# Zero-tile matmuls in TensorE's waits, a new order of the norm columns, and a value product in row halves

## What is computed

```
x_dct = DCT over w and h of the normalised x
blocks of 8 x 8 frequencies, 64 of them per image:
    q, k, v = tokens @ Wq, Wk, Wv          (4 heads of 16)
    q, k    = each divided by its norm over the block's 64 positions
    attn    = softmax(q k^T * rescale);  x_low = (attn v) @ proj_w + proj_b
h1     = gelu(1x1 conv(x_dct)); h1 = gelu(3x3 depthwise conv(h1)); x_conv = h1 + x_dct
x_high = gelu(1x1 conv(x_conv)) + x_conv
x      = x + inverse DCT(coef * x_low + (1 - coef) * x_high + x_dct)
t      = tokens of x (4096 of 64 numbers), layer norm
router = softmax(t @ Wr + br), top 2 of 8 experts, weights from their gap
t      = t + sum over experts of gate * (gelu(LN(t) @ W1 + b1) @ W2 + b2)
```

## Time and profile before

| | before |
|---|---|
| median of three executions | 278.15 us (277.07 to 278.45) |
| the profiled execution | 280.61 us, its span 278.4 us |
| TensorE busy | 247.1 us, 89% of the span |
| VectorE, ScalarE, GpSimd busy | 53%, 47%, 16% |
| mean granted clock of TensorE | 0.936 of full speed |
| DMA | 13.42 MB, 48 GB/s over the span |

### The profile page before, as it was taken

How to read it: one execution, slowest core, us unless ns; L and a number is a source line. 1 busy time by engine, 2 the same in 40 slices (tenths; PEclk the granted TensorE clock), 3 DMA queues, 4 the chain that set the end, 5 groups by cost and what they waited for, 6 DMA issues and landing times.

```text
span 278.4 us, 3222 instructions
## 1 busy us (share of the span) xinstructions
PE 247.1 (89%) x1238; PEld 134.8 (48%) x1238; DVE 146.7 (53%) x264; ACT 130.2 (47%) x206; POOL 45.4 (16%) x45
## 2 busy tenths in 40 slices
PE   3678789999996796896898979999999999999994
PEld 3564579956844464596795223222232333333331
DVE  0780938884359797187597344433344433334444
ACT  1336641003062244405616746555665665666660
POOL 3930067003085006400330000000000000000000
PEclk9955999999999799998955999999999999999998
DMA  7920000000000000000000861507060523215000
GB/s 242 237 44 0 2 0 4 0 0 0 2 0 0 1 0 0 2 0 0 2 0 13 181 129 46 105 0 190 0 151 2 128 60 93 61 55 133 1 2 38
DMA packets 6143, 13.42 MB, mean 48 GB/s; under 512 B 2672, under 2 KB 4080, under 8 KB 5104
## 3 DMA queue, kind: packets, MB, share of 16 engines
q1 hardware_dynamic: 6128, 13.21, 20.1%
HBM read 12.03 MB, written 1.18 MB: 47 GB/s over the span
## 4 chain that ended last, share of the span: by engine, by line
PE 70%; DVE 16%; ACT 6%; DMA 5%; issue 1%; SPq 0%; DVEq 0%
PE psum L636 21%; PE psum L621 20%; PE psum L451 5%; PE psum L469 3%; PE psum L441 3%; PE psum L513 3%; DMA wide<-gate_store 3%; DVE place L978 2%; PE psum L408 2%; PE psum L538 2%; PE psum L477 2%; PE psum L391 2%; DVE place L962 2%; ACT place L671 1%; PE psum L556 1%
## 5 line engine op out<-in xcount | busy, mean ns | idle before, releaser
L778 ACT ACTIVATE hid<-psum,b1p 128x512 f32<-128x512 f32 x128 | 77.9, 688 | 43.3 <-PE psum L621 43.3
L621 PE MATMUL psum<-tok,w1s 128*128 128x512 f16 x256 | 64.7, 390 | 0.0
L636 PE MATMUL psum<-hid,w 128*64 128x512 f32 x256 | 61.8, 604 | 2.0 <-DVE term L1062 2.0
L1062 DVE SCALAR_TENSOR_TENSOR term<-psum,sm,wide 128x512 f32<-128x512 f32 x32 | 24.0, 750 | 73.0 <-PE psum L636 68.0
L621 PEld LDWEIGHTS psum<-tok,w1s 128*128 128x128 f16 x256 | 21.9, 100 | 51.3 <-ACT hid L778 26.6
L636 PEld LDWEIGHTS psum<-hid,w 128*64 128x64 f32 x256 | 15.6, 136 | 34.0 <-issue 26.6
L1067 DVE TENSOR_TENSOR x<-x,term 128x512 f32<-128x512 f32 x32 | 22.1, 692 | 1.1
L469 PE MATMUL psum<-h_pad,tap_bd 128*128 128x512 f32 x36 | 15.8, 592 | 0.0
L451 PE MATMUL psum<-wide,c 128*128 128x128 f32 x64 | 14.4, 396 | 0.0
L451 PEld LDWEIGHTS psum<-wide,c 128*128 128x128 f32 x64 | 13.1, 205 | 1.3 <-issue 0.5
L906 DVE SCALAR_TENSOR_TENSOR place<-h_pad,sm,place 128x512 f32<-128x512 f32 x16 | 12.0, 752 | 0.6
(11 more groups left out here) (135 smaller groups left out, 325.8 us busy)
## 6 DMA issues: line engine op xcount, KB each, us to landing
wide<-gate_store SPq DMA_DIRECT2D x16, 512.0 KB, 6.3
xs<-in_x SPq DMA_DIRECT2D x2, 512.0 KB, 5.0
w1f<-in_W SPq DMA_DIRECT2D x2, 512.0 KB, 8.9
block_out<-x SPq DMA_DIRECT2D x4, 256.0 KB, 6.6
w<-in_W SPq DMA_DIRECT2D x1, 512.0 KB, 11.2
c<-const SPq DMA_DIRECT2D x1, 483.5 KB, 4.3
sm<-in_small SPq DMA_DIRECT2D x1, 419.0 KB, 5.2
gate_store<-gate_rows SPq DMA_DIRECT2D x2, 64.0 KB, 5.5
```

The costliest lines, as they stand in the source:

```text
L621: mm = pe.matmul(h_bank(n), w1s[:, part, e, k * P:(k + 1) * P], tok[:, pair, half, b, :], start=part == 0, stop=part == 1)
L636: mm = pe.matmul(y_bank(u)[b * H:(b + 1) * H, :], w2[:, e * KT + k, :], hid[:, u % 2, B2 * k + b, :], start=k == 0, stop=k == KT - 1)
L778: act.activation(hid[:, u % 2, t, :], h_bank(n), ACT.Gelu, bias=b1p[:, e * KT + k:e * KT + k + 1]).then_inc(gelu_ready, 1)
L1062: dve.scalar_tensor_tensor(term[:, u % 2, :], y_bank(u), b2t[:, e:e + 1], gate_b[part][:, e % (E // 2), :], ALU.add, ALU.mult).then_inc(te ...
```

## The change

There are three edits.

**Holds.** A tile `still` of 128 x 512 fp16 is zeroed as GpSimd's first instruction. `hold_clock(count, where)` on TensorE issues `count` matmuls of that tile with itself, 512 columns each, into a bank that holds nothing needed at that point. They stand ahead of the waits of `dct_over_h` (7 for pair 0, after a wait for the zeroed tile, 6 for pair 1), `dct_over_w(0)` (8), `windows(0)` (6), `conv_in(0)` (6), `norms_of_k(1)` (8, with its two waits in the other order and the holds between them), `inverse_over_kh(1)` (6), both `features` (5 each) and both `gates_to_rows` (5 each). The last have new waits ahead of the holds: for the normalised tokens, and for pair 0 also for `bias_ready`, since the bank is the one in which the sums of `bias` lie.

**Norm columns.** The columns of Wq and Wk were ordered (which, head, depth), and are now ordered (depth, which, head). With that `prod` has the eight columns of one depth side by side, and `norms` reads runs of eight floats, 128 apart, where it read single floats 16 apart. ScalarE's `keep_tk` now reads PSUM with a step of eight floats, and `diagonal` for `wq_bd` reads its source with such a step.

**Value product.** `wv_rep` holds Wv on all rows, 128 x 128 in place of two such tiles, and `times_wv` multiplies the lower 64 rows and the upper 64 rows by themselves, each into its bank, where it multiplied all 128 rows with zeros in one half.

```diff
@@ -117,7 +117,7 @@
 
 SMALL = {}
 at = 0
-for name, n in (("wqk", 2 * HD), ("proj", HEADS * C), ("c1a", C), ("c2", C), ("wv_t", 2 * C), ("taps", 9), ("proj_b", 1),
+for name, n in (("wqk", 2 * HD), ("proj", HEADS * C), ("c1a", C), ("c2", C), ("wv_t", C), ("taps", 9), ("proj_b", 1),
                 ("rescale", HEADS), ("ln_g", E), ("ln_b", E), ("b1", NT), ("b2", E), ("wr", E), ("br", E),
                 ("coef", H * K)):
     SMALL[name] = slice(at, at + n)
@@ -132,14 +132,12 @@
     def put(name, v):
         v = v.reshape(v.shape[0], -1)
         out[:, SMALL[name]] = np.tile(v, (P // v.shape[0], 1))
-    put("wqk", np.concatenate([a["L0_conv_Wq"], a["L0_conv_Wk"]], axis=1))
+    both = np.stack([a["L0_conv_Wq"].reshape(C, HEADS, DH), a["L0_conv_Wk"].reshape(C, HEADS, DH)], axis=1)
+    put("wqk", both.transpose(0, 3, 1, 2))
     put("proj", a["L0_conv_proj_w"].reshape(HEADS, DH, C).transpose(1, 0, 2))
     put("c1a", a["L0_conv_c1a_w"].reshape(C, C).T)
     put("c2", a["L0_conv_c2_w"].reshape(C, C).T)
-    wv = np.zeros((2, HD, 2, C), np.float32)
-    for odd in range(2):
-        wv[odd, :, odd] = a["L0_conv_Wv"].T
-    put("wv_t", wv.reshape(P, 2 * C))
+    put("wv_t", a["L0_conv_Wv"].T)
     put("taps", a["L0_conv_c1b_w"].reshape(C, 9))
     put("proj_b", a["L0_conv_proj_b"].reshape(C, 1))
     put("rescale", a["L0_conv_rescale"].reshape(1, HEADS))
@@ -194,7 +192,7 @@
 
         def weight(name):
             return sm[:, SMALL[name]]
-        wqk = weight("wqk").rearrange("p (a n) -> p a n", a=2)
+        wqk = weight("wqk")
         proj = weight("proj").rearrange("p (h c) -> p h c", h=HEADS)
         c1a, c2, wv_t, taps_w = weight("c1a"), weight("c2"), weight("wv_t"), weight("taps")
         lng, lnb, b1t, b2t = weight("ln_g"), weight("ln_b"), weight("b1"), weight("b2")
@@ -203,7 +201,7 @@
         proj_bd = sb("proj_bd", [P, HEADS, P])
         conv_bd = sb("conv_bd", [P, 4, P])
         tap_bd = sb("tap_bd", [P, 9, P])
-        wv_rep = sb("wv_rep", [P, 2, P])
+        wv_rep = sb("wv_rep", [P, P])
         coef_rest = sb("coef_rest", [P, CHUNK])
         w1f = sb("w1f", [P, E, HID])
         w1g = sb("w1g", [P, E, HID])
@@ -216,6 +214,7 @@
         xs = sb("xs", [P, PAIRS, N])
         x1 = sb("x1", [P, PAIRS, N])
         tok = sb("tok", [P, PAIRS, 2, B2, TT // 2 * P], F16)
+        still = sb("still", [P, CHUNK], F16)
         gate_rows = sb("gate_rows", [P, PAIRS, P])
         h_pad = sb("h_pad", [P, PAIRS, B2, H + 2, K + 2])
         place = [sb(f"place{n}", [P, PAIRS, N]) for n in range(6)]
@@ -246,7 +245,7 @@
         spread_k = [wide[0][:, p, 0:N] for p in range(PAIRS)]
         y_sb = [wide[0][:, p, 0:N] for p in range(PAIRS)]
         y_t = [wide[0][:, p, N:2 * N] for p in range(PAIRS)]
-        prod = [wide[1][:, p, :].rearrange("p (g a n) -> p g a n", a=2, n=HD) for p in range(PAIRS)]
+        prod = [wide[1][:, p, :].rearrange("p (g n) -> p g n", n=P) for p in range(PAIRS)]
         mix = [wide[1][:, p, :].rearrange("p (g n) -> p g n", n=P) for p in range(PAIRS)]
 
 
@@ -290,6 +289,7 @@
         const_in, const16_in, weights_in = sem("const_in"), sem("const16_in"), sem("weights_in")
         ffn_in, out_done = sem("ffn_in"), sem("out_done")
         dve_chain, pool_chain = sem("dve_chain"), sem("pool_chain")
+        still_zero = sem("still_zero")
         pad_zero, bd_ready, w1_ready = sem("pad_zero"), sem("bd_ready"), sem("w1_ready")
         conv_bd_ready = sem("conv_bd_ready")
         bias_t, bias_ready, wr_ready = sem("bias_t"), sem("bias_ready"), sem("wr_ready")
@@ -373,8 +373,18 @@
         def _(pe):
 
 
+            def hold_clock(count, where):
+
+                for _ in range(count):
+                    pe.matmul(where, still[:, 0:P], still[:, 0:where.shape[1]], start=True, stop=True)
+
             def dct_over_h(p):
 
+                if p == 0:
+                    pe.wait_ge(still_zero, 1)
+                    hold_clock(7, bank(slot(1, 1), 0))
+                if p:
+                    hold_clock(6, bank(slot(1, 1), 0))
                 pe.wait_ge(x_in[p], 16)
                 pe.wait_ge(dct_in, 16)
                 for cp in range(CP):
@@ -384,6 +394,8 @@
 
             def dct_over_w(p):
 
+                if p == 0:
+                    hold_clock(8, bank(slot(1, 1), 0))
                 pe.wait_ge(const_in, 16)
                 for cp in range(CP):
                     if cp % 4 == 0:
@@ -434,11 +450,10 @@
             def gram_times_w(p):
 
                 pe.wait_ge(weights_in, 16)
-                wqk_all = wqk[:, :, :].rearrange("p a n -> p (a n)")
                 for g in range(G):
                     if g % K == 0:
                         pe.wait_ge(gram_ready, 2 * p + g // K + 1)
-                    mm = pe.matmul(slot(p, g // K)[:, g % K * P:(g % K + 1) * P], gram[p][:, parity(g), :], wqk_all, start=True, stop=True)
+                    mm = pe.matmul(slot(p, g // K)[:, g % K * P:(g % K + 1) * P], gram[p][:, parity(g), :], wqk, start=True, stop=True)
                     if g % K == K - 1:
                         mm.then_inc(t_done, 1)
 
@@ -446,9 +461,9 @@
 
                 pe.wait_ge(tk_ready, 2 * p + 1)
                 pe.wait_ge(prod_ready, 2 * (p + 1))
-                columns = prod[p].rearrange("p g a (h d) -> p d (g a h)", d=DH)
+                columns = prod[p].rearrange("p g (d n) -> p d g n", d=DH)
                 for d in range(DH):
-                    mm = pe.matmul(slot(p, 0)[:, 0:2 * G * HEADS], const("pick")[:, DH - 1 - d:DH - 1 - d + P], columns[:, d, :],
+                    mm = pe.matmul(slot(p, 0)[:, 0:2 * G * HEADS], const("pick")[:, DH - 1 - d:DH - 1 - d + P], columns[:, d, :, :],
                                    start=d == 0, stop=d == DH - 1)
                 mm.then_inc(norms_done, 1)
 
@@ -471,8 +486,10 @@
 
             def norms_of_k(p):
 
+                pe.wait_ge(second_dconv_ready, p + 1)
+                if p:
+                    hold_clock(8, bank(slot(p, 0), 1))
                 pe.wait_ge(spread_ready, p + 1)
-                pe.wait_ge(second_dconv_ready, p + 1)
                 for j in range(2):
                     mm = pe.matmul(slot(p, 0)[:, j * CHUNK:(j + 1) * CHUNK], mask, spread_k[p][:, j * CHUNK:(j + 1) * CHUNK],
                                    start=True, stop=True)
@@ -510,8 +527,9 @@
                 for j in range(2):
                     pe.wait_ge(yt_ready, 2 * p + j + 1)
                     for odd in range(2):
-                        mm = pe.matmul(slot(p, j)[:, odd * CHUNK:(odd + 1) * CHUNK], wv_rep[:, odd, :],
-                                       y_t[p][:, j * CHUNK:(j + 1) * CHUNK], start=True, stop=True)
+                        of = slice(odd * HD, (odd + 1) * HD)
+                        mm = pe.matmul(slot(p, j)[:, odd * CHUNK:(odd + 1) * CHUNK], wv_rep[of, :],
+                                       y_t[p][of, j * CHUNK:(j + 1) * CHUNK], start=True, stop=True)
                     mm.then_inc(mix_done, 1)
 
             def low(p):
@@ -533,6 +551,8 @@
 
             def inverse_over_kh(p):
 
+                if p:
+                    hold_clock(6, bank(slot(0, 1), 0))
                 pe.wait_ge(back_ready, 2 * (p + 1))
                 for cp in range(CP):
                     mm = pe.matmul(slot(p, 0)[:, cp * P:(cp + 1) * P], back[p][:, cp * P:(cp + 1) * P], idct_h, start=True, stop=True)
@@ -559,6 +579,7 @@
 
             def features(p):
 
+                hold_clock(5, bank(slot(p, 1), 0))
                 pe.wait_ge(const16_in, 16)
                 to = slot(p, 1).bitcast(F16)
                 for j in range(TT):
@@ -585,6 +606,11 @@
 
             def gates_to_rows(p):
 
+                pe.wait_ge(xn_ready, 2 * (p + 1))
+                if p == 0:
+                    pe.wait_ge(bias_ready, 1)
+                pe.wait_ge(xn_ready, 2 * (p + 1))
+                hold_clock(5, bank(slot(p, 0), 1))
                 pe.wait_ge(gparts_ready, p + 1)
                 pe.transpose(slot(p, 0)[:, P:2 * P], gates[:, p].rearrange("p j b e t -> p (j b e t)"), ident).then_inc(gates_done, 1)
 
@@ -693,7 +719,7 @@
                 for j in range(2):
                     act.wait_ge(prod_ready, 2 * p + j + 1)
                     act.copy(tk[p].rearrange("p (h g e) -> p g h e", h=HEADS, e=DH)[:, j * K:(j + 1) * K, :, :],
-                             slot(p, j).rearrange("p (g a h e) -> p g a h e", a=2, h=HEADS, e=DH)[:, :, 1, :, :]).then_inc(tk_ready, 1)
+                             slot(p, j).rearrange("p (g e a h) -> p g a h e", a=2, h=HEADS, e=DH)[:, :, 1, :, :]).then_inc(tk_ready, 1)
 
             def gelu_depthwise(p):
                 act.wait_ge(first_taps_done, p + 1)
@@ -786,6 +812,7 @@
 
         @block.gpsimd
         def _(pool):
+            pool.memset(still[:, :], 0.0).then_inc(still_zero, 1)
             pool.memset(h_pad[:, :, :, :], 0.0).then_inc(pad_zero, 1)
             pool.wait_ge(const_in, 16)
             pool.wait_ge(weights_in, 16)
@@ -801,14 +828,12 @@
```

(12 more changed lines are left out.)

## The result

The changed kernel took 269.53 us (four executions, 268.1 to 272.17) where the kernel before took 277.61 on the same chip (277.02 to 278.45): a ratio of 0.969, 95% interval 0.9635 to 0.9744. The forecast was 267.3 with a range of 263.5 to 272.0. The ratio leaves out the slow execution of 272.17 us; the medians take all. Measured beside other kernels on a second chip it came to 0.9684 (0.9616 to 0.9751). So the gain is about 8.6 us by the ratio (8.1 in the medians of the first chip, 9.4 in those of the second), a fifth less than the 10.9 of the sum.

What follows compares the result with a forecast made beforehand. It took a chain of some 40 short stages, partly at 1.2 GHz, then the gates' latency as the bound. Terms summed to -10.9 us, from 280.61 to 269.7; less the 2.5 us median offset, 267.3, range 263.5 to 272.

Steps and rivals of the forecast that it cites:

- signs of being wrong: Holds where no wait was, the clock falling between 14 and 100 us, or VectorE late for norms_of_k(0).
- Start: Holds up to pair 0's first convolution: -0.4 us in the first product, -3.4 us from product over w to windows(0).
- Norm columns: Both norms stages: runs of eight floats end the slow spaced reads, 3.3 us per pair, all on the path, -6.5 us.
- norms_of_k(1): Eight holds in its 3.63 us wait for VectorE: -1.3 us there, -0.2 in the transposes behind, -1.5 us.
- Value product: times_wv in halves, from 3.60 to 1.9 us: 0 for pair 0, -1.1 us at low for pair 1.
- rival 2: Clock falls in a gap without holds, such as ahead of to_frequencies(0): 271.3 us, chance 0.15.
- inverse_over_kh(1): Six holds in its 2.51 us wait: -1.0 us there, -0.35 in the product over kw behind, -1.35 us.
- Features and gates: Cold holds and new waits at features and gates_to_rows(0) delay the gates' transpose: +3.35 us.
- the last one of the sum: Whole kernel: the profiled execution's 2.5 us over the median carried over, taking 269.7 to 267.3 us.
- Rival 1: Clock stays up through bias, which halves, and gates run at +1.15: 265.1 us, chance 0.15.
- nor did 3: At all holds: matmuls of zeros do not hold the clock, all clock gains gone, 280.4 us, chance 0.05.
- or 4: In norms: 16 accumulations into one bank, not spacing, make it slow; 6.5 us lost, 273.8 us, chance 0.05.

Runs made afterwards that it cites:

- norms_only: The kernel before with the new norm columns alone: 273.69 us, ratio 0.9792 to the kernel before.
- start_holds: The kernel before plus norm columns, value product in halves and only the five groups of holds up to pair 0's first convolution: 266.93 us, ratio 0.9543.
- small_ones: The changed kernel without its holds, plus 33 matmuls of the zeroed tile with eight columns ahead of x: 269.29 us, ratio 0.9633.
- the two kernels on spacing: The kernel before with norms reading other columns of prod, contiguous or in runs of two and four floats: one execution each, 270.24 and 270.69 us.

## Why the prediction was right, and where it was off

The time lies in the range, and for the start, the norm columns, the inverse and the gates the steps went as worked out. That the sum fits the two profiled executions is luck, since two terms failed and a gain outside the sum covered them. The prediction also named signs of being wrong, and one came true: the clock fell between 14 and 100 us, at 82.0 and at 92.2. Holds without a wait stood in `features` and `gates_to_rows(0)`, where the sum had priced them. By its steps:

1. **Start**, forecast -0.4 and -3.4. The first gram product moved from 37.48 to 33.71, -3.8. Right in the trace; the first product did profit only at its end (3.1 us for 3.78). Its size is an average over chance: 2.5 to 3.2 us over the executions, as worked out above.
2. **Norm columns**, -6.5. Both stages shrank by 6.8 together (7.16 and 6.99 to 3.77 and 3.57), and all of it reached the path: `norms_of_k(1)` came 10.6 us earlier, 3.8 from the start and 6.8 from here. VectorE was not late. The ratio of norms_only gives 5.8, its median 5.2; right, if a little too good. (The tap row makes 0.22 us per 128 columns, not 0.21; nothing hangs on it.)
3. **norms_of_k(1)**, -1.5: got -0.15. This is the step that failed. "Eight holds of 0.24 are 1.9, inside the wait" was true, and not enough: I took filling half of the wait as holding the clock. The row shows 1.92 us idle behind them and the fall. With 15 holds, which leave 0.40 us, the product took 1.98 in both traces.
4. **Value product**, -1.1: -0.8 for pair 1 (`to_frequencies(0)` to `to_frequencies(1)`: 9.87 ahead, then 10.67). The product took 1.99 for 3.60, as the gram rows said; of the drain that the Trainium skill (TensorEngine Tiling (Array Packing), Key Properties) names, without a figure, no more shows than the 0.19 us by which this exceeds half of 3.60. "For pair 0 VectorE is late anyway: 0" missed what a shorter product in front of a late VectorE does: it lengthens the idling. Together with the rest of the stretch the path lost 0.85 there (`to_frequencies(0)` 9.87 ahead, where the softmax before it was 10.72 ahead). That is rival 2, in another gap than the one I named, and it came from a part of the change. Other traces bear this out: of the eight with the halves and no holds ahead of `low(0)`, six had 1.8 to 2.2 us of idling there and the clock fell in `low(0)`; two had 1.6, and it did not. In the four with the old product the idling is 0.5 us at most and the clock did not fall there. So in pair 0 the stretch cost 0.85, where the sum had 0.
5. **inverse_over_kh(1)**, -1.35: -1.6. The product took 2.05 us for 3.04. That the holds kept the clock up fits all six traces with them, but without them it also stayed up in two of eight (start_holds and small_ones, 2.05 us behind 2.5 of idling), so part of this term is chance.
6. **Features and gates**, +3.35: the start of the transpose fell back from 12.25 ahead to 8.76, +3.5. All its pieces came as worked out: the clock fell within router and bias, both batches of five were cold (2.3 each, where 2.1 and 1.8 were forecast), and the first batch delayed `features(1)`. The run without these holds says 4.5 by the ratios and 3.4 to 3.8 in the medians, and the trace says 3.5: they agree as far as the noise allows.
7. **What was not on the list**: the moved fetch, -2 us at the store. With it the first `term` stood 10.9 us ahead although the transpose was only 8.8 ahead. After it the five holds of `gates_to_rows(1)`, which I had put into a wait of 2 us, stand in the chain at 147.6 with 1.2 us. They cost next to nothing all the same: the first `term` ended at 150.6 and `down(1)` started at 150.66, so without them TensorE would have waited for it.

The sum came out at the profile's 10.86 only because items 3 and 4 (2.5 us too good together) were offset by item 7 and smaller ones. Against the ratio it is 2.3 us too good. The step behind this is the last one of the sum, which carried the 2.5 us between the profiled execution and the median over to the changed kernel. Before the change they stand 3.0 us apart (280.61 and 277.61), after it 0.2 (269.75 and 269.53). The profiled execution before had a mean granted clock of 0.936. Of the 25 executions of the kernel before that ran beside the experiments, the six with 0.931 or 0.932 took 279.7 to 280.9 us and the eight with 0.960 to 0.969 took 276.5 to 278.5. So the sum was worked out against an execution of low clock, in which holds have more to gain than in most. Rival 1 did not happen (the clock fell in bias), nor did 3 (zeros bring the clock up: at 6.9 us in place of 10.5) or 4 (the two kernels on spacing). The failed steps are 3, the pair 0 part of 4, and this carrying over.

## What to carry to other kernels

A matmul put into a wait is free only if the wait is really there when it runs, at the clock that holds then; ahead of the one instruction that a long latency path waits for, leave the engine idle. Filling half of a wait may buy nothing, and making a stage faster in front of a late engine opens a new gap. Let fp32 columns that TensorE streams lie in pairs at least. When a change adds instructions, compare the times of short DMAs on the path as well: 2 us came and went here with where a fetch of instructions fell. A sum worked out on one profiled execution holds for that execution: see first how far it lies from the median, and whether the change removes the reason.

## What the runs showed of the hardware

- DMA packets of 16 KB and 0.9 to 1.5 us, read here as fetches of TensorE's instructions, come once for about 250 of its records. A 64 KB store on the path took 1.6 us without one (eight traces) and 2.8 to 3.6 with one in it (six). Adding 66 records ahead moved it.
- The same idling of 1.9 us ahead of `norms_of_k(1)` was followed by the lower clock in three traces (3.08 us and more for its product) and not in a fourth (1.99).
- After 2.5 us of idling ahead of `inverse_over_kh(1)` the clock fell in six of eight traces, where the product took 2.56 to 3.56 us, and not in two, where it took 2.05.
- Router and bias, few columns to a matmul, count as busy in the profile (12.75 of 13.65 us in the earlier trace rows), and the clock fell in them at 140.25 before the change and at 129.8 after.
- With seven matmuls of 512 zeros ahead of the first product the clock came up at 4.8 to 7.0 us in seven traces; without, at 8.7 to 27.3 in seven, one of which had 33 matmuls of eight columns there (17.6).
- A matmul of 128 single fp32 columns takes 0.447 us at the higher clock, about what contiguous ones take at the lower (eight in 3.78, 0.47 each); in runs of two or more it takes 0.234.
